# Four attention layers on one core: layer 2's transposed scores from rounded operand parts, with the maxima added in a pass of their own

## The chip, the core and the metric

The kernel runs on one core of a Trainium2 chip. The core has a matrix engine (TensorE, PE in the profile; PEld is its weight load), a vector engine (VectorE, DVE), an activation engine (ScalarE, ACT), a general engine (GpSimd, POOL) and an engine that issues DMAs (SyncE, SP). They run side by side and wait for each other through semaphores. The metric is the device time of one execution in microseconds (us); lower is better. SBUF is the on-chip memory that all engines read, PSUM the memory that TensorE writes its products to.

## The reference

Four attention layers in a row, each on x of shape (2, 128, 32, 32), that is, per image b a matrix of 128 channels by N = 1024 positions, each with a residual.

```python
# layer 0: 4 heads of 4 dims, softmax over the query positions (axis -2)
S = einsum('bhdn,bhdm->bhnm', q, k);  A = softmax(S, axis=-2)
x = gamma * (Wo @ (v A) + bo) + x
# layer 1: one head of 16 dims, v has 128 channels
x = x + gamma * (v @ softmax(q k)^T)
# layer 2: 8 heads of 16 dims; k, v from a 2x2 average pool (256 positions)
q = wq @ group_norm(x);  kvn = group_norm(avg_pool2(x));  k, v = wk @ kvn, wv @ kvn
attn = softmax(einsum('bhdq,bhdk->bhqk', q, k) * 16 ** -0.5)
x = x + wproj @ (attn v)
# layer 3: one head of 128 dims, group norm with 32 groups, biases
x = x + out_w @ softmax(q k^T * 128 ** -0.5) v + out_b
```

## The kernel before

**Steps.** The work is cut into steps that stand in one list, the plan: a string of letters, ORDER (L93 to L104), is read from left to right, and each letter takes the next step of its kind. All engines walk the same list, each doing its own part of a step, in order. So the string sets what stands behind what on every engine. The kinds:

- A: plain scores of one tile (TensorE), whose negated row maxima VectorE takes (L663 for layer 2, L666 for layer 0, L669 for layers 1 and 3).
- top: after eight A tiles the maxima are transposed (L910), copied by ScalarE (L528), and a DMA issued by SyncE puts them as rows beside or among the score operands.
- B: transposed scores of one tile with the maxima subtracted by the product itself (L918 layer 0, L923 layer 1, L929 layer 2, L933 layer 3), whose exponential ScalarE writes to one of the NP = 13 probability buffers (L539, 128x1024).
- PV4 (layers 0 and 2, four 32-column products side by side, L960, two B tiles a step) and PV1 (layers 1 and 3, L966, half a tile a step): values times probabilities, added up in one PSUM accumulator.
- N, V: q, k, v projections and the group norm steps; E, Y: sums' reciprocals (den), their broadcast (bcast), the output product (y).

**Units.** Layer 0 has four head-group units per image, layer 2 two, layers 1 and 3 one. Units of image 0 and image 1 and of neighbouring layers overlap: while image 0 changes layer, TensorE works on image 1, and the other way round.

**PSUM.** Products go to a ring of three tiles of 1024 columns (RING = 3); step n waits until the reader of step n - 3 has read. So TensorE runs at most three tiles ahead of VectorE and ScalarE.

**Number formats.** TensorE takes float32 operands (each multiply is shown as two records in the trace) or operands that were rounded on being written (fp32r; one record). A product of full accuracy can be had from rounded operands by splitting each into its rounded part and the rest. Layers 0 and 1 do so (SPLIT = (0, 1)): ScalarE writes the rounded part with a sign and mask to a staging buffer (HT, two of them, L491), VectorE adds it to the product (L630), and rows of the operand hold now the rounded part and now the rest. Layers 2 and 3 keep two copies instead: fp32r rows (RA, RB, KR2) for the A tiles, float32 rows (FA, FB, KF2) for the B tiles.

**Layer 2 in detail.** q comes in two halves of heads (g = 0, 1), each copied by ScalarE to RA or RB (L494) and by VectorE to FA or FB (L636). k is written twice per copy, once for each parity of heads, with the other parity's rows masked to zero (L472 on ScalarE to KR2, L616 on VectorE to KF2; two instructions of 512 columns each). A B tile (L929) is two float32 multiplies, one on rows 0 to 63 and one on rows 64 to 127 of the array, 512 columns each: 32 such tiles, 64 multiplies. The maxima stand in row ONE of each 32-row group of FA and FB, and masked k has a 1 there (one2k), so that the first B tile of a unit waits for their DMA (L914).

**Layers 1 and 3.** After the B tile's products a pass of its own adds the maxima: two fp32r multiplies of 64 rows and 512 columns, max_picker times max_half_rows (L941). In layer 3 the products before it are four records of 128 rows (L933).

**Vector and scalar work between layers.** From the update of x to the first A tile of layer 2 there is one chain: statistics (L755 to L762), averages over groups (L1024), the coefficients (L769 to L801), the normalized x (L580), q and k products (L845, L849, L832), the copies, the first A tile (L892).

## Time and profile before

| | |
|---|---|
| time, median of 3 runs | 370.57 us (369.66 to 370.78) |
| the profiled execution | 369.77 us, span of the core 367.6 us |
| TensorE busy | 339.6 us, 92% |
| VectorE busy | 246.5 us, 67% |
| ScalarE busy | 192.3 us, 52% |
| GpSimd busy | 52.0 us, 14% |

The span is the time from the first to the last instruction that the profile shows; the rest of the execution's time, 2.2 us, lies around it. Busy time of TensorE counts a matmul to its modelled end, so two that follow each other overlap in the trace, and the distance between the starts is what a matmul costs in a run of them.

### The profile page before, as it was taken

How to read it: one execution, taken by the hardware profiler on the slowest of the kernel's cores; microseconds unless marked ns; L12 is line 12 of the kernel's file. 1: busy time of each engine (PE TensorE's matmuls, PEld its weight loads, DVE VectorE, ACT ScalarE, POOL GpSimd, SP SyncE). 2: the span in 40 equal slices, each digit the busy share in tenths (PEclk: the TensorE clock that was granted, in tenths of full speed). 3: DMA queues.
4: the chain of work that ended last, by engine and by line, in shares of the span. 5: the costliest groups of instructions: out<-in, count | busy, mean ns of one | idle time of the engine just before them, and what ended most of it. 6: DMA issues, size and time to landing. Idle time of an engine off the chain costs nothing.

```text
span 367.6 us, 4597 instructions
## 1 busy us (share of the span) xinstructions
PE 339.6 (92%) x1766; PEld 147.7 (40%) x1766; DVE 246.5 (67%) x325; ACT 192.3 (52%) x235; POOL 52.0 (14%) x37
## 2 busy tenths in 40 slices
PE   8888989899899996899999999979999999999995
PEld 5343223333434442344343445534443343643441
DVE  2889796778889857498867437986981153890543
ACT  4454678877673477736556535237147725214310
POOL 5000000000006600000000425003210021005700
PEclk9885899999999999899999999999999999999999
DMA  7000000000000000000000000000000000000101
GB/s 295 30 0 2 0 3 1 0 2 0 2 0 2 0 0 2 2 2 2 0 4 0 2 0 0 2 0 1 3 2 4 0 0 2 0 0 2 57 0 57
DMA packets 1436, 4.43 MB, mean 12 GB/s; under 512 B 168, under 2 KB 520, under 8 KB 1288
## 3 DMA queue, kind: packets, MB, share of 16 engines
q1 hardware_dynamic: 1416, 4.15, 3.0%
q8 instruction: 14, 0.23, 0.3%
q14 instruction: 6, 0.05, 0.0%
HBM read 2.99 MB, written 1.05 MB: 11 GB/s over the span
## 4 chain that ended last, share of the span: by engine, by line
PE 74%; DVE 17%; ACT 4%; issue 4%; DVEq 0%; ACTq 0%
PE attn_acc L966 13%; PE attn_acc L960 11%; DVE neg_max L666 7%; PE products L933 7%; PE products L929 6%; PE products L918 5%; PE products L845 4%; PE products L879 4%; PE products L849 4%; PE products L857 3%; PE products L892 3%; PE products L941 2%; PE products L1015 2%; DVE neg_max L669 2%; ACT probs L539 2%
## 5 line engine op out<-in xcount | busy, mean ns | idle before, releaser
L539 ACT ACTIVATE probs<-products 128x1024 f32<-128x1024 f32 x128 | 126.9, 1025 | 86.2 <-PE products L941 50.1
L666 DVE TENSOR_REDUCE neg_max<-products 128x2 f32<-128x1024 f32 x64 | 75.9, 1219 | 14.8 <-PE products L879 14.4
L966 PE MATMUL attn_acc<-probs,v 128*128 128x512 f32 x128 | 64.0, 614 | 0.1
L960 PE MATMUL attn_acc<-probs,v 128*32 128x512 f32 x384 | 50.3, 612 | 0.1
L393 POOL TENSOR_TENSOR prob_sum<-prob_sum,probs 128x1024 f32<-128x1024 f32 x16 | 37.7, 2358 | 66.4 <-ACT probs L539 65.8
L669 DVE TENSOR_REDUCE neg_max<-products 128x1 f32<-128x1024 f32 x32 | 37.8, 1219 | 8.6 <-PE products L884 6.6
L393 POOL TENSOR_TENSOR prob_sum<-probs 128x1024 f32<-128x1024 f32 x4 | 9.4, 2360 | 229.9 <-ACT probs L539 229.9
L663 DVE TENSOR_REDUCE neg_max<-products 128x4 f32<-128x1024 f32 x32 | 37.7, 1219 | 4.1 <-PE products L892 3.6
L933 PE MATMUL products<-rows_a,rows_b 128*128 128x512 f32 x64 | 31.3, 611 | 0.5 <-ACT v L518 0.3
L966 PEld LDWEIGHTS attn_acc<-probs,v 128*128 128x128 f32 x128 | 21.8, 189 | 20.9 <-issue 17.1
L684 DVE RECIPROCAL recips<-products 128x128 f32<-128x128 f32 x10 | 9.6, 956 | 21.7 <-PE products L986 21.6
L918 PE MATMUL products<-rounded_a,q_even 64*128 64x512 f32 x64 | 16.7, 520 | 2.9 <-DVE neg_max L666 2.2
L879 PE MATMUL products<-q_even,rounded_a 64*128 64x512 f32 x64 | 16.3, 524 | 1.8 <-DVE neg_max L666 1.1
L563 ACT ACTIVATE attn_out<-attn_acc 128x512 f32<-128x512 f32 (+1 forms) x15 | 11.9, 792 | 10.8 <-PE attn_acc L960 8.2
L929 PE MATMUL products<-rows_a,k_rows 64*128 64x512 f32 x64 | 16.4, 610 | 0.4 <-DVE neg_max L663 0.4
L933 PEld LDWEIGHTS products<-rows_a,rows_b 128*128 128x128 f32 x64 | 11.2, 189 | 12.7 <-issue 11.4
L879 PE MATMUL products<-rounded_b,rounded_a 64*128 64x512 f32 x64 | 14.3, 453 | 1.0 <-ACT probs L539 0.7
L960 PEld LDWEIGHTS attn_acc<-probs,v 128*32 128x32 f32 x384 | 8.5, 109 | 16.3 <-issue 11.3
L929 PE MATMUL products<-rows_b,k_rows 64*128 64x512 f32 x64 | 14.9, 599 | 0.0
L918 PE MATMUL products<-rounded_a,rounded_b 64*128 64x512 f32 x64 | 14.2, 466 | 0.6 <-DVE neg_max L666 0.5
L941 PE MATMUL products<-max_half_rows,max_picker 64*128 64x512 f32 x64 | 14.3, 442 | 0.0
L580 ACT ACTIVATE x_norm<-x,norm_scale_shift 128x512 f32<-128x512 f32 x8 | 6.1, 806 | 13.1 <-DVE norm_scale_shift L779 13.1
(140 smaller groups left out, 388.1 us busy)
## 6 DMA issues: line engine op xcount, KB each, us to landing
w<-w_rest SPq DMA_DIRECT2D x1, 1236.5 KB, 7.6
x<-x SPq DMA_DIRECT2D x2, 512.0 KB, 4.6
tmp<-row_selector SPq DMA_DIRECT2D x1, 512.0 KB, 8.4
y<-x SPq DMA_DIRECT2D x1, 512.0 KB, 2.6
y<-x SPq DMA_DIRECT2D x2, 256.0 KB, 2.0
w<-w_first SPq DMA_DIRECT2D x1, 147.0 KB, 2.2
rounded_a<-max_rows SPq DMA_DIRECT2D x8, 4.0 KB
max_half_rows<-max_rows SPq DMA_DIRECT2D x4, 4.0 KB
```

The costliest lines, as they stand in the source:

```text
L393: engine.tensor_tensor(DS[:, :], first_in, P[:, n % NP, :], ALU.add).then_inc(den_acc, 1)
L539: nc.scalar.activation(P[:, n % NP, :], slot(s), ACT.Exp, scale=SCALE[L]).then_inc(read_act, 1)
L663: nc.vector.tensor_reduce(out=m2, in_=slot(s).rearrange("p (a i k) -> p a i k", a=2, i=2), op=ALU.max, axis=AX.X, negate=True).then_inc(re ...
L666: nc.vector.tensor_reduce(out=m[:, 2 * t:2 * t + 2], in_=slot(s).rearrange("p (a n) -> p a n", a=2), op=ALU.max, axis=AX.X, negate=True).t ...
L669: nc.vector.tensor_reduce(out=m[:, t:t + 1], in_=slot(s), op=ALU.max, axis=AX.X, negate=True).then_inc(read_dve, 1)
L879: mm = nc.tensor.matmul(slot(s)[:, halves[a]], RA[b][rows, tile], q0_parity(b, g // 2)[rows, halves[nh]], start=True, stop=True)
L918: mm = nc.tensor.matmul(slot(s)[:, halves[a]], q0_parity(b, g // 2)[rows, 128 * t:128 * (t + 1)], RA[b][rows, halves[g % 2]], start=True, ...
L929: mm = nc.tensor.matmul(slot(s)[:, halves[a]], KF2[b][rows, hp, g, 128 * kt:128 * (kt + 1)], (FA, FB)[g][b][rows, halves[half]], start=Tru ...
L933: nc.tensor.matmul(slot(s)[:, h], FB[b][:, 128 * t:128 * (t + 1)], FA[b][:, h], start=True, stop=False)
L941: mm = nc.tensor.matmul(slot(s)[:, h], pick[rows, :], MR[b][rows, :], start=False, stop=True)
L960: mm = nc.tensor.matmul(acc[32 * j:32 * j + 32, h], lhs, P[:, b_no[q] % NP, halves[a]], start=t0 == 0 if L == 0 else t0 % 2 == 0, stop=t0 ...
L966: mm = nc.tensor.matmul(acc[:, h], V13[b][:, t0, :], P[:, b_no[q] % NP, h], start=t0 == first, stop=t0 == last)
```

## The change

**Layer 2's B tiles.** SPLIT takes in layer 2. The q and k rows now hold each 16-dim head twice in its 32-row group: the rounded part and the rest. k is stored in two versions for each parity (KS[b], versions v = 0, 1), with the parts in the one and in the other order, so that the sum of both products is the whole product. A B tile is four fp32r multiplies of 64 rows and 512 columns, and then two more, max_picker times the rows of maxima (MR, MR1), which add the maxima: six instead of two, all fp32r. The wait for the maxima's DMA stands between the fourth and the fifth. The A tiles use version 0.

**Staging.** For q (each half of heads) ScalarE writes the negated rounded part to HT and VectorE adds it to the product. For k ScalarE writes four pieces of 512 columns (parity times version) instead of two, and VectorE writes four instead of two. VectorE's first waits for ScalarE's last. ScalarE waits, before it writes to one of the two HT buffers, until VectorE has read what was there two stagings before (k counts as two).

**Layer 3.** The maxima are written as one row of 1024 (row 2) instead of two half rows, and the pass that adds them is two multiplies of all 128 rows, one for each half of the columns, instead of two of 64 rows each.

**Constants.** max_picker comes by a DMA (192 KB more) and is rounded by ScalarE in the fold step, instead of being set by GpSimd.

**Buffers.** Probability buffers 12 instead of 13, output buffers 4 instead of 5.

**Order.** ORDER is a new string.

```diff
-SPLIT = (0, 1)
-NP = 13
+SPLIT = (0, 1, 2)
+PARITIES = 2
+NP = 12
-O_TILES = 5
+O_TILES = 4
...
-    "BPPBBEBPNBPBBNPPBPNNBPBABAPBAPAVAPAPAEAETNEBBABBAB"
+    "BPPBBEBBPNBBNPBPNNBBPPPPABAPBAAVAPAPAEAETNEBBBABAP"
...
-                        for p in range(2):
-                            masked = nc.scalar.activation(KR2[b][:, p, :, :].rearrange("p g n -> p (g n)"),
-                                                          slot(s)[:, 0:2 * NKV], ACT.Identity,
-                                                          scale=w("group_mask")[:, p:p + 1],
-                                                          bias=w("one2k")[:, p:p + 1])
+                        for p in range(PARITIES):
+                            at = staged.index(s) + p
+                            if at >= 2:
+                                wait_read(act, staged[at - 2])
+                            for v, h in enumerate(halves):
+                                i = PARITIES * v + p
+                                hi = nc.scalar.activation(HT[:, at % 2, h], slot(s)[:, 0:2 * NKV], ACT.Identity,
+                                                          scale=w("s2k")[:, i:i + 1])
...
-                        for p in range(2):
-                            masked = nc.vector.tensor_scalar(KF2[b][:, p, :, :].rearrange("p g n -> p (g n)"),
-                                                             slot(s)[:, 0:2 * NKV], w("group_mask")[:, p:p + 1],
-                                                             w("one2k")[:, p:p + 1], ALU.mult, ALU.add)
+                        for p in range(PARITIES):
+                            for v, h in enumerate(halves):
+                                lo = nc.vector.scalar_tensor_tensor(
+                                    out=KS[b][:, v, p, :, :].rearrange("p g n -> p (g n)"), in0=slot(s)[:, 0:2 * NKV],
+                                    scalar=w("group_mask")[:, p:p + 1] if PARITIES == 2 else 1.0,
+                                    in1=HT[:, (staged.index(s) + p) % 2, h].bitcast(F32), op0=ALU.mult, op1=ALU.add)
...
-                            mm = nc.tensor.matmul(slot(s)[:, halves[a]], KF2[b][rows, hp, g, 128 * kt:128 * (kt + 1)],
-                                                  (FA, FB)[g][b][rows, halves[half]], start=True, stop=True)
+                            for v in range(2):
+                                nc.tensor.matmul(slot(s)[:, halves[a]], KS[b][rows, v, hp, g, 128 * kt:128 * (kt + 1)],
+                                                 (RA, RB)[g][b][rows, halves[half]], start=v == 0, stop=False)
+                        if t == 0:
+                            pe.wait_ge(consts_act, 1)
+                            pe.wait_ge(maxrows_in[b], max_count(L, b, g))
+                        for a in range(2):
+                            rows = slice(WIDE * a, WIDE * a + WIDE)
+                            mm = nc.tensor.matmul(slot(s)[:, halves[a]], pick[rows, hp, :], (MR[b], MR1)[g][rows, halves[half]],
+                                                  start=False, stop=True)
...
-                            rows = slice(WIDE * i, WIDE * i + WIDE)
-                            mm = nc.tensor.matmul(slot(s)[:, h], pick[rows, :], MR[b][rows, :], start=False, stop=True)
+                            rows = slice(WIDE * i, WIDE * i + WIDE) if L == 1 else slice(0, 128)
+                            mm = nc.tensor.matmul(slot(s)[:, h], pick[rows, 0 if L == 1 else 2, :],
+                                                  MR[b][rows, 0:HALF] if L == 1 else MR[b][:, h], start=False, stop=True)
```

In the rows of order below, a name before the arrow is written and those behind it are read, sizes are partitions x columns, and x8 means eight of them in a row; v13_0 are values of image 0 in layers 1 and 3, v0_1 and v2_1 those of image 1 in layers 0 and 2.

**Place 1**, TensorE, second unit of layer 2's image 1 (its last B tiles). Before:

```order
L960 MATMUL attn_acc<-probs,v2_1 32x512 x4
L910 MATMUL products<-w2,neg_max 32x128
L929 MATMUL products<-rows_a1,k2_rows1 128x512 x6
L960 MATMUL attn_acc<-probs,v2_1 32x512 x12
L929 MATMUL products<-rows_b1,k2_rows1 128x512 x16
L986 MATMUL products<-attn_out4,w2 32x128 x8
```

After:

```order
L984 MATMUL attn_acc<-probs,v2_1 32x512 x8
L945 MATMUL products<-rounded_b1,k2_rows1 128x512 x4
L952 MATMUL products<-max_rows_odd,max_picker 128x512 x2
L945 MATMUL products<-rounded_b1,k2_rows1 128x512 x4
L952 MATMUL products<-max_rows_odd,max_picker 128x512 x2
L945 MATMUL products<-rounded_b1,k2_rows1 128x512 x4
L952 MATMUL products<-max_rows_odd,max_picker 128x512 x2
L984 MATMUL attn_acc<-probs,v2_1 32x512 x4
```

Eight B tiles in a row are now broken up by a PV4 step, and each is six instructions.

**Place 2**, TensorE, image 0's entry to layer 2, from the averages of its statistics to its first A tile (k2_rounded0 or k2_rows0); L918 and L933 are B tiles of layer 0's image 1, 128x512 x2 each. Before:

```order
L1024 MATMUL products<-mean_var,w2 128x4
L960 MATMUL attn_acc<-probs,v0_1 32x512 x8
L918 MATMUL products<-rounded_a1,rounded_b1 128x512 x2
L845 MATMUL products<-x_norm,w2 128x512
L849 MATMUL products<-x_norm,w2 128x512
L832 MATMUL products<-kv_norm,w2 128x256 x2
L918 MATMUL products<-rounded_a1,rounded_b1 128x512 x2
L960 MATMUL attn_acc<-probs,v0_1 32x512 x4
L918 MATMUL products<-rounded_a1,rounded_b1 128x512 x2
L892 MATMUL products<-k2_rounded0,rounded_a0 128x256 x4
```

After:

```order
L1048 MATMUL products<-mean_var,w2 128x4
L984 MATMUL attn_acc<-probs,v0_1 32x512 x4
L933 MATMUL products<-rounded_a1,rounded_b1 128x512 x2
L984 MATMUL attn_acc<-probs,v0_1 32x512 x4
L860 MATMUL products<-x_norm,w2 128x512
L864 MATMUL products<-x_norm,w2 128x512
L847 MATMUL products<-kv_norm,w2 128x256 x2
L933 MATMUL products<-rounded_a1,rounded_b1 128x512 x4
L984 MATMUL attn_acc<-probs,v0_1 32x512 x12
L907 MATMUL products<-k2_rows0,rounded_a0 128x256 x4
```

Three PV4 steps stand now between the k product and the first A tile, where one stood.

**Place 3**, image 1's entry to layer 2, TensorE; L933 (before) and L956 (after) are B tiles of layer 3's image 0. Before:

```order
L1024 MATMUL products<-mean_var,w2 128x4
L966 MATMUL attn_acc<-probs,v13_0 128x512
L933 MATMUL products<-rows_a0,rows_b0 128x512 x2
L941 MATMUL products<-max_half_rows0,max_picker 128x512 x2
L966 MATMUL attn_acc<-probs,v13_0 128x512
L845 MATMUL products<-x_norm,w2 128x512
L849 MATMUL products<-x_norm,w2 128x512
L832 MATMUL products<-kv_norm,w2 128x256 x2
L845 MATMUL products<-x_norm,w2 128x512
L849 MATMUL products<-x_norm,w2 128x512
L933 MATMUL products<-rows_a0,rows_b0 128x512 x2
L941 MATMUL products<-max_half_rows0,max_picker 128x512 x2
```

After:

```order
L1048 MATMUL products<-mean_var,w2 128x4
L956 MATMUL products<-rows_a0,rows_b0 128x512 x2
L964 MATMUL products<-max_rows_of0,max_picker 128x512 x2
L990 MATMUL attn_acc<-probs,v13_0 128x512
L860 MATMUL products<-x_norm,w2 128x512
L864 MATMUL products<-x_norm,w2 128x512
L847 MATMUL products<-kv_norm,w2 128x256 x2
L990 MATMUL attn_acc<-probs,v13_0 128x512 x3
L860 MATMUL products<-x_norm,w2 128x512
L864 MATMUL products<-x_norm,w2 128x512
L907 MATMUL products<-k2_rows1,rounded_a1 128x256 x4
L956 MATMUL products<-rows_a0,rows_b0 128x512 x2
```

Three PV1 steps moved in behind the k product, and the B tile of layer 3 that stood ahead of the first A tile (L892, which follows the last row of before) stands now behind it (L907). On VectorE the same place is, before:

```order
L636 COPY rows_a1<-products 128x512 x2
L616 TENSOR_SCALAR k2_rows1<-products,w1,w2 128x512 x2
L636 COPY rows_b1<-products 128x512 x2
L663 TENSOR_REDUCE neg_max<-products 128x2x2 x16
L684 RECIPROCAL recips<-products 128x128
```

and after:

```order
L642 SCALAR_TENSOR_TENSOR rounded_a1<-products,stage_hi 128x512 x2
L627 SCALAR_TENSOR_TENSOR k2_rows1<-products,w1,stage_hi 128x512 x4
L642 SCALAR_TENSOR_TENSOR rounded_b1<-products,stage_hi 128x512 x2
L678 TENSOR_REDUCE neg_max<-products 128x2x2 x16
L699 RECIPROCAL recips<-products 128x128
```

Ahead of the sixteen maxima stand eight instructions instead of six.

## Rows read from the trace of the kernel before

**Rows 1.** The page: busy time by engine; chain that ended last.

```profile
PE 339.6 (92%) x1766; PEld 147.7 (40%) x1766; DVE 246.5 (67%) x325; ACT 192.3 (52%) x235; POOL 52.0 (14%) x37
...
PE 74%; DVE 17%; ACT 4%; issue 4%; DVEq 0%; ACTq 0%
```

**Rows 2.** Windows: length; busy us (instructions) of PE, PEld, DVE, ACT, POOL; granted clock; DMA.

```profile
0.00:40.00 40.00, 34.48 (x128) 16.81 (x128) 28.56 (x36) 19.38 (x26) 4.79 (x17) 0.79 0.20 75
...
320.00:367.60 47.60, 42.86 (x149) 17.65 (x148) 21.61 (x22) 10.68 (x12) 11.76 (x5) 0.99 0.06 22
```

**Rows 3.** Timeline of PE, layer 2's last eight B tiles: start us, us, instructions.

```profile
283.21 7.14 PE L929 MATMUL products<-rows_b,k_rows 64*128 64x512 f32 x32
290.27 0.64 PE L986 MATMUL products<-attn_out,w 128*32 128x128 f32 x16
```

**Rows 4.** The same, records alive at 283.25 and at 284.0.

```profile
283.21 0.70 PE L929 MATMUL products<-rows_b,k_rows 64*128 64x512 f32 x2
...
283.74 0.59 PE L929 MATMUL products<-rows_b,k_rows 64*128 64x512 f32 x2
```

**Rows 5.** Timeline of PE, fp32r multiplies of 64 rows, a pair each row.

```profile
109.77 0.50 PE L879 MATMUL products<-rounded_b,rounded_a 64*128 64x512 f32 x2
110.11 0.39 PE L923 MATMUL products<-rounded_a,rounded_b 64*128 64x512 f32 x2
110.34 0.39 PE L941 MATMUL products<-max_half_rows,max_picker 64*128 64x512 f32 x2
110.57 0.39 PE L879 MATMUL products<-rounded_b,rounded_a 64*128 64x512 f32 x2
```

**Rows 6.** Timeline of PE, B tiles of layer 3 in the last unit.

```profile
345.39 1.98 PE L933 MATMUL products<-rows_a,rows_b 128*128 128x512 f32 x4
347.31 0.50 PE L941 MATMUL products<-max_half_rows,max_picker 64*128 64x512 f32 x2
347.74 1.99 PE L933 MATMUL products<-rows_a,rows_b 128*128 128x512 f32 x4
```

**Rows 7.** Timeline of PE, fp32r multiplies of 128 rows beside float32 ones.

```profile
224.94 1.36 PE L897 MATMUL products<-rounded_b,rounded_a 128*128 128x512 f32 x4
226.13 1.02 PE L966 MATMUL attn_acc<-probs,v 128*128 128x512 f32 x2
```

**Rows 8.** Timeline, image 0's entry to layer 2.

```profile
151.03 1.45 ACT L472 ACTIVATE k_rounded<-products,w 128x512 fp32r<-128x512 f32 x2 [1.11 <-PE products L832]
...
152.58 1.53 DVE L616 TENSOR_SCALAR k_rows<-products,w 128x512 f32<-128x512 f32 x2 [1.87 <-ACT k_rounded L472]
154.26 0.50 PE L892 MATMUL products<-k_rounded,rounded_a 64*128 64x256 f32 x4 [1.22 <-DVE k_rows L616]
```

**Rows 9.** Durations by line (ns, min/median/max): staging and copies of 512 columns.

```profile
L630 DVE SCALAR_TENSOR_TENSOR rounded_a<-products,w,stage_hi x8: 750/751/751, 7.4 to 176.8; 128x512 fp32r<-128x512 f32 x8
...
L494 ACT ACTIVATE rounded_a<-products x4: 581/593/598, 148.6 to 251.0; 128x512 fp32r<-128x512 f32 x4
...
L496 ACT ACTIVATE rounded_a<-products,w x4: 671/684/687, 220.9 to 312.1; 128x512 fp32r<-128x512 f32 x4
```

**Rows 10.** Timeline, image 1's entry to layer 2.

```profile
253.39 1.88 PE L933 MATMUL products<-rows_a,rows_b 128*128 128x512 f32 x4
253.43 1.53 DVE L616 TENSOR_SCALAR k_rows<-products,w 128x512 f32<-128x512 f32 x2 [1.03 <-ACT k_rounded L472]
...
255.54 0.40 PE L892 MATMUL products<-k_rounded,rounded_a 64*128 64x256 f32 x4
...
256.07 5.83 DVE L663 TENSOR_REDUCE neg_max<-products 128x4 f32<-128x1024 f32 x5
```

**Rows 11.** Windows with the granted clock, at both entries to layer 2.

```profile
145.00:149.00 4.00, 2.26 (x4) 1.01 (x5) 1.08 (x5) 3.22 (x5) 0.00 (x0) 0.87 0.00 0
149.00:153.00 4.00, 4.00 (x17) 1.64 (x15) 1.80 (x3) 2.75 (x5) 0.00 (x0) 0.70 0.01 2
240.00:257.00 17.00, 14.48 (x46) 6.48 (x48) 12.27 (x35) 9.05 (x14) 2.51 (x2) 1.00 0.00 1
```

More of the change, by code:

```diff
@@ L156, in build_plan, with attention_layers @@
     return [next(following[c]) for c in ORDER]
-def attention_layers(nc, x, first, rest, sel, out):
+def attention_layers(nc, x, first, rest, sel, picker, out):
     plan = build_plan()
@@ L345, in max_count @@
             order = [s for s in top_no if s[2] == b]
-            return 16 * sum(MAX_DMAS[s[1]] for s in order[:order.index(("top", L, b, g)) + 1])
+            return 16 * (order.index(("top", L, b, g)) + 1)
         def acc_free(L, b, g):
@@ L1072 @@
     group_mask = np.zeros((2, 2, GROUP, 2), np.float32)
[L1073 removed]
+    s2 = np.zeros((2, 2, 2, D2, 2, PARITIES), np.float32)
     for p in range(2):
         group_mask[:, p, :, p] = 1
[L1076 removed]
+    for v in range(2):
+        for p in range(PARITIES):
+            s2[:, slice(p, p + 1) if PARITIES == 2 else slice(0, 2), 1 - v, :, v, p] = -1
+    s2q = np.zeros((4, 2, D2, 1), np.float32)
+    s2q[:, 1] = -1
+    picker = np.zeros((2, 2, GROUP, 3, C), np.float32)
+    for p in range(2):
+        picker[:, p, 0, p] = 1
+    picker[0, 0, 2, 2] = 1
     w0o = np.zeros((4, 32, 2, 2, 32), np.float32)
```

114 lines of the change are left out of this document (60 added, 54 removed), and 1 row of the table REST.

## The prediction

> **What bounds the kernel now.** I read the page first: TensorE is busy 92% of the span and makes 74% of the chain that ended last; VectorE has 17% of that chain [rows 1]. The windows then show where TensorE is not enough of an answer: in the first 40 us it is busy 34.5 us at a granted clock of 0.79, in the last 47.6 us it is busy 42.9 us at 0.99 [rows 2]. So what TensorE is spared or given counts nearly in full from layer 2 on, except at the entries to a layer, where one chain through VectorE and ScalarE runs and TensorE lives on the other image's tiles. The change touches both: the price of B tiles, and the chain at the two entries to layer 2.
>
> **Layer 2's B tiles, removed work.** Eight B tiles (32 records, four a tile) start at 283.21 and the next step starts at 290.27 [rows 3]: 7.06 / 8 = 0.88 us a tile. In the records, two start together at 283.21 and two at 283.74 [rows 4]. The first distance, 0.53, holds a load that a wait kept back; the rest of the run is then (7.06 - 0.53) / 15 = 0.435 for a pair. So a tile is two slots of 0.43, 0.86 in a run and 0.96 after a wait.
>
> **The same, added work.** Six fp32r multiplies, three on each half of the array's rows. Pairs of that kind start at 110.11, 110.34 and 110.57, 0.23 apart, and 0.34 after the first pair, which had waited [rows 5]. If they pair up, a tile is 3 x 0.23 = 0.69 in a run and 0.34 + 2 x 0.23 = 0.80 after a wait. That is 0.16 less, times 32 tiles = **-5.1 us**. The pairing is the question, since the code gives both products of rows 0 to 63 before those of rows 64 to 127. The float32 tile answers it: there too one multiply, with both its records, stands ahead of the other half's, and yet the trace shows one record of each half starting together [rows 4]. I take three slots. Four slots, 0.92, would be +0.06 a tile; that is a rival below. The wait for the maxima moves from ahead of the tile to behind four of its multiplies; as the unit's first tile waits for a DMA, that can hide at most 0.46 in each of four units, and I count nothing.
>
> The Trainium skill ("TensorE: Matmul & The Clock Gate", Part 3, What overlaps and what doesn't) has matmuls start and end strictly in program order. By that rule a float32 tile alone would need three slots, a0, a0 with a1, a1, and the two pairs of rows 4 would not be seen; the new tile would take four slots whenever the next step is not one on half the rows (six of the 32 in the new order: 1.4 us given back). The trace speaks against the rule here, and the sum above doesn't use it.
>
> **Layer 3's maxima.** From one tile to the next it is 347.74 - 345.39 = 2.35 us [rows 6]. Four float32 records of all rows at 0.43 are 1.72, so the pass on half the rows costs 0.63, though its pair alone would be 0.23: the change between the array's two shapes costs 0.40, once in and once out. After the change both multiplies use all rows and follow each other. Four such start at 224.94 and the next step at 226.13 [rows 7]: 0.30 each with the first one's wait in it, 0.23 without. A tile is then 1.72 + 0.46 = 2.18 (2.32 by the 0.30), 0.17 less. Where the next step uses half the rows anyway (four of sixteen tiles before, two in the new order), the change of shape is only put off. I take 14 tiles x 0.17 = -2.4, plus two at +0.2: **-2.0 us**; between -2.7 and 0.
>
> **Image 0's entry to layer 2** (place 2). ScalarE writes the two k pieces from 151.03 to 152.48, VectorE from 152.58 to 154.11, and the first A tile starts at 154.26 after 1.22 us of waiting [rows 8]. Now there are four and four. For ScalarE a piece with a scale but no bias has no row: it lies between 0.593 (neither) and 0.684 (bias alone), and two such pieces overlap as those in the 1.45 do [rows 8, 9]. Four at 0.63 are 2.5, +1.05. For VectorE the same instruction as L630 is 0.751 [rows 9]; four with the overlap seen in rows 8 are 2.85, +1.3. The chain is 2.35 longer. Cover: one PV4 step, two slots of 0.43, more stands ahead of the first A tile than before (six between the update of x and that tile, for five), and is missing after it. Net **+1.5 us**. Between +0.7, if PSUM's ring lets TensorE use more of what it has, and +3, if it waits again for what it did early. One PV4 step less stands ahead of the averages (place 2), so that a gap opens there earlier; it is part of this sum.
>
> **Image 1's entry** (place 3). The k copies end at 253.43 + 1.53 = 254.96, the first A tile starts at 255.54 and the maxima at 256.07, and five of them take 5.83, some 1.13 apart [rows 10]. With the chain 2.35 longer the k rows are there at 257.3, so the A tile is 1.8 late. Ahead of it TensorE has done two PV1 steps more (1.7) and one layer 3 tile less (2.18): +0.5. Then a wait that the change adds: ScalarE stages q's second half in the HT buffer that k's first parity used, so it waits for VectorE's last k piece; VectorE's next instruction waits for that. 257.3 + 0.7 + 2 x 0.75 = 259.5 for the first of sixteen maxima instead of 256.07. Behind it wait the ring of three tiles and TensorE's A tiles; sixteen maxima at 1.13 would end at 277.6. I add 0.2 for the ring: **+2.5 us**, between +1.5 and +3.5.
>
> **Order and buffers.** Counting, in both orders, changes between steps on all rows, half the rows and 32-column groups, with layer 3's maxima taken as all rows in both: 184 and 191. Seven more at about 0.2 (half of the 0.40 above) are 1.4; half of them I take to fall where TensorE waits anyway: **+0.7**, between -1 and +2. Fewer buffers: in the new order no exponential needs a buffer whose PV step stands less than ten steps ahead of it, and no output buffer is asked for before its last reader is over 80 steps past: nothing. With one more wait of ScalarE on PV in image 0's last layer 0 tiles, 1 us at most. The larger constant DMA is issued after all that the start needs, and its rounding is one short instruction in the fold step: nothing.
>
> **The sum.** -5.1 - 2.0 + 1.5 + 2.5 + 0.7 = -2.4 us. The profiled execution would go from 369.77 to 367.4, and the median, which lay 0.8 above it, from 370.57 to **368.2 us**.
>
> **The rivals.**
> 1. *The gain is only half there.* Image 1's A tiles pace TensorE by VectorE's maxima (1.13 each), and the last B tiles by ScalarE. For it: five maxima without a gap [rows 10]. Against it: 92% busy [rows 1]. If layer 2's tiles give 2.6 instead of 5.1: 370.57 + 0.1 = 370.7 us.
> 2. *The entries cost more* (the slower side). Both are at their upper ends, 3 + 3.5 = 6.5 instead of 4.0, and the longer idleness brings the clock down. At image 0's entry TensorE was busy 2.26 of 4 us and the granted clock fell to 0.87 and then 0.70, that is, part of the time on the lower of its two levels (1.2 instead of 2.4 GHz); at image 1's entry it stayed at 1.00 [rows 11]. The price of that fall was 0.3 x 4 + 0.13 x 4 = 1.7 us. Idle a little longer at image 1's entry, and it is paid there too: -2.4 + 2.5 + 1.7 = +1.8, 372.4 us. [...] Against it: B tile and PV1 steps fill most of it.
> 3. *Four slots instead of three.* 32 x 0.23 = 7.4 more than the sum: 375.6 us. Against it speak rows 4.
> 4. *The new order hides the entries.* Places 2 and 3 show work moved to where the chain is longer; if it all counts, the +4.7 for entries and order shrink to 1: 364.5 us.
> 5. *It doesn't do what it says.* The multiplies are fp32r on rounded operands as in layers 0 and 1, whose trace rows exist; I see no way for that, and give it nothing.
>
> **How the numbers follow.** The forecast, 366.8 to 369.3, has 0.48; rival 1 has 0.23, rival 2 0.15, rival 3 0.05, rival 4 0.09. A difference under 0.3% (1.1 us) can't be told from no change. Faster by more than that are the forecast, rival 4 and a little of rival 1: 0.58. Within it is most of rival 1 and a little of rival 2: 0.23. Slower: rival 3, most of rival 2, a little of rival 1: 0.19. The range takes in half of rival 4 and rival 2: 365.0 to 372.2.
>
> **What would show it.** The B tiles of layer 2 in a run: starts of tiles 0.69 apart, records in three pairs 0.23 apart (four distances if rival 3 holds). Layer 3's tiles 2.18 apart. The four k pieces: 2.5 us on ScalarE and 2.85 on VectorE at both entries, and the first A tiles 2.35 later after the k product. On VectorE at image 1's entry a gap of about 0.7 between k's last piece and q's first. TensorE's busy time should fall by some 5 to 7 us, and its idle time rise by about 4. The prediction is wrong if the granted clock falls at a second place, if rows show four slots, or if the stretch before image 0's entry, which the change hardly touches, differs by over 1 us by the new order alone.

## The result, and the profile after

The changed kernel takes 373.3 us (median of 5 runs, 372.5 to 374.57) where before takes 369.66 (median of 5 beside them, the three runs of the first median among them): ratio 1.0092, 95% interval 1.0070 to 1.0115, some 3.4 us slower. Another six runs gave 373.84, ratio 1.0104 (1.0075 to 1.0132), which is 3.8 us. The forecast was 368.2 us and its range ended at 372.2. The profiled execution took 373.17 us with a span of 370.7, where before has 369.77 and 367.6: +3.1 in the span.

The page of the changed kernel, busy time by engine (beside rows 1):

```profile
PE 337.1 (91%) x1830; PEld 157.7 (43%) x1830; DVE 245.1 (66%) x329; ACT 194.9 (53%) x240; POOL 53.1 (14%) x35
```

TensorE is busy 2.5 us less, and idle 33.6 us (370.7 - 337.1) for 28.0 before: 5.6 more. So its work did get less, but by half or less of the 5 to 7 us that the prediction had named as a sign, and more than that turned into waiting.

**Where it went.** The table cuts the span at ends of single instructions that all these kernels have: a layer's first or last row maxima on VectorE and a layer's last exponential on ScalarE. Each column is one profiled execution. The mark (c) says that TensorE's granted clock fell once in that stage; the low clock of the first 42 us, which every trace has and which lies in stages a and b, and the fall in the last 6 us are not marked. E2's two falls straddle the ends of the stages c and e. The other columns are experiments, told below: E1 (new order, old steps), E2 (old order, new steps), E9 and E10 (new steps with k's second version copied by DMA, in the old order and in the new).

| stage, us | before | after | E1 | E2 | E9 | E10 |
|---|---|---|---|---|---|---|
| a. start to first maxima, image 0 | 12.5 | 13.5 | 13.1 | 12.5 | 13.2 | 12.6 |
| b. to the last layer 0 maxima of image 1 | 116.2 | 118.0 | 119.0 (c) | 116.6 | 117.0 | 118.7 (c) |
| c. image 0's entry, to layer 2's first maxima | 27.3 (c) | 27.1 | 26.6 (c) | 28.5 (c) | 25.8 | 26.8 (c) |
| d. to the last layer 3 maxima of image 0 | 83.2 | 82.3 | 83.2 | 83.6 | 82.3 | 82.3 |
| e. image 1's entry, to layer 2's first maxima | 18.1 | 21.3 (c) | 19.3 | 21.2 | 18.3 | 19.5 |
| f. to the last layer 2 exponential | 34.5 | 33.9 | 35.9 | 35.1 (c) | 34.0 | 34.3 |
| g. to the last layer 3 exponential | 59.4 | 59.6 | 61.7 | 58.4 | 59.4 | 59.5 |
| h. to the end | 16.4 | 15.1 | 15.3 | 16.2 | 16.2 | 15.1 |
| span | 367.6 | 370.7 | 374.0 | 372.1 | 366.2 | 368.9 |

A new order also moves work across these cuts, so single stages of kernels with different orders compare only roughly. The stages with layer 2's B tiles (d and f) gained 0.9 and 0.6 where 5.1 in all was forecast, image 1's entry lost 3.2, and stage b, before layer 2, lost 1.7 (117.96 for 116.24).

**The tiles themselves came out as forecast.** Timeline of TensorE in the changed kernel, layer 2's last unit (L945 the products, L952 the maxima):

```profile
285.52 0.63 PE L945 MATMUL products<-rounded_b,k_rows 64*128 64x512 f32 x4
285.98 0.40 PE L952 MATMUL products<-max_rows_odd,max_picker 64*128 64x512 f32 x2
286.21 0.63 PE L945 MATMUL products<-rounded_b,k_rows 64*128 64x512 f32 x4
286.67 0.41 PE L952 MATMUL products<-max_rows_odd,max_picker 64*128 64x512 f32 x2
```

286.21 - 285.52 = 0.69 a tile: three slots, for 0.88 in rows 3. Layer 3 (beside rows 6):

```profile
334.76 1.88 PE L956 MATMUL products<-rows_a,rows_b 128*128 128x512 f32 x4
336.08 1.03 PE L964 MATMUL products<-max_rows_of,max_picker 128*128 128x512 f32 x2
336.95 0.59 PE L956 MATMUL products<-rows_a,rows_b 128*128 128x512 f32 x1
```

336.95 - 334.76 = 2.19, forecast 2.18.

**Image 1's entry** (beside rows 10), VectorE and ScalarE:

```profile
256.11 2.73 DVE L627 SCALAR_TENSOR_TENSOR k_rows<-products,w,stage_hi 128x512 fp32r<-128x512 f32 x4 [1.91 <-ACT stage_hi L482]
259.71 1.29 DVE L642 SCALAR_TENSOR_TENSOR rounded_b<-products,stage_hi 128x512 fp32r<-128x512 f32 x2 [0.88 <-issue]
260.92 1.21 DVE L678 TENSOR_REDUCE neg_max<-products 128x4 f32<-128x1024 f32 x1
```

```profile
253.57 2.42 ACT L482 ACTIVATE stage_hi<-products,w 128x512 fp32r<-128x512 f32 x4 [0.17 <-PE products L847]
258.93 1.27 ACT L499 ACTIVATE stage_hi<-products,w 128x512 fp32r<-128x512 f32 x2 [2.93 <-DVE k_rows L627]
```

ScalarE's four k pieces take 2.42 (forecast 2.5), VectorE's four 2.73 (2.85). ScalarE then waits 2.93 until VectorE has read the last k piece, and VectorE stands 0.88 before q's second half (0.7). This is the wait through the staging buffer that the prediction described. At image 0's entry the same pieces and TensorE's wait, beside rows 8:

```profile
151.38 2.42 ACT L482 ACTIVATE stage_hi<-products,w 128x512 fp32r<-128x512 f32 x4 [0.18 <-PE products L847]
```

```profile
153.91 2.73 DVE L627 SCALAR_TENSOR_TENSOR k_rows<-products,w,stage_hi 128x512 fp32r<-128x512 f32 x4 [1.91 <-ACT stage_hi L482]
```

```profile
156.78 0.50 PE L907 MATMUL products<-k_rows,rounded_a 64*128 64x256 f32 x4 [1.52 <-DVE k_rows L627]
```

### The profile page after: what moved, and what is told of

The parts are those of the page before. It is cut to its first block and busy times, and to the rows that moved or that the text cites. A ratio compares the mean times of both kernels' runs of the same rounds, so it can differ in the third digit from the quotient of the medians.

```text
span 370.7 us, 4743 instructions
## 1 busy us (share of the span) xinstructions
PE 337.1 (91%) x1830; PEld 157.7 (43%) x1830; DVE 245.1 (66%) x329; ACT 194.9 (53%) x240; POOL 53.1 (14%) x35
## 5 line engine op out<-in xcount | busy, mean ns | idle before, releaser
L684 DVE TENSOR_REDUCE neg_max<-products 128x1 f32<-128x1024 f32 x32 | 37.9, 1220 | 10.2 <-PE products L899 7.0
L956 PE MATMUL products<-rows_a,rows_b 128*128 128x512 f32 x64 | 32.4, 631 | 0.8 <-DVE neg_max L678 0.6
L964 PE MATMUL products<-max_rows_of,max_picker 64*128 64x512 f32 (+1 forms) x64 | 23.0, 497 | 0.1
L699 DVE RECIPROCAL recips<-products 128x128 f32<-128x128 f32 x10 | 9.5, 954 | 19.7 <-PE products L1010 19.5
L393 DVE TENSOR_TENSOR prob_sum<-prob_sum,probs 128x1024 f32<-128x1024 f32 x8 | 9.8, 1220 | 19.1 <-POOL prob_sum L393 18.4
L933 PE MATMUL products<-rounded_a,q_even 64*128 64x512 f32 x64 | 16.0, 508 | 3.7 <-DVE neg_max L681 2.5
L933 PE MATMUL products<-rounded_a,rounded_b 64*128 64x512 f32 x64 | 14.7, 472 | 2.5 <-ACT probs L549 2.1
L956 PEld LDWEIGHTS products<-rows_a,rows_b 128*128 128x128 f32 x64 | 11.8, 194 | 12.0 <-issue 9.8
L984 PEld LDWEIGHTS attn_acc<-probs,v 128*32 128x32 f32 x384 | 8.3, 109 | 15.1 <-issue 11.8
L933 PEld LDWEIGHTS products<-rounded_a,q_even 64*128 64x128 f32 x64 | 6.5, 200 | 16.1 <-DVE neg_max L681 9.4
L964 PEld LDWEIGHTS products<-max_rows_of,max_picker 64*128 64x128 f32 (+1 forms) x64 | 9.3, 192 | 8.9 <-issue 8.7
```

Source lines behind the costliest of these rows:

```text
L393: engine.tensor_tensor(DS[:, :], first_in, P[:, n % NP, :], ALU.add).then_inc(den_acc, 1)
L684: nc.vector.tensor_reduce(out=m[:, t:t + 1], in_=slot(s), op=ALU.max, axis=AX.X, negate=True).then_inc(read_dve, 1)
L933: mm = nc.tensor.matmul(slot(s)[:, halves[a]], q0_parity(b, g // 2)[rows, 128 * t:128 * (t + 1)], RA[b][rows, halves[g % 2]], start=True, ...
L956: nc.tensor.matmul(slot(s)[:, h], FB[b][:, 128 * t:128 * (t + 1)], FA[b][:, h], start=True, stop=False)
L964: mm = nc.tensor.matmul(slot(s)[:, h], pick[rows, 0 if L == 1 else 2, :], MR[b][rows, 0:HALF] if L == 1 else MR[b][:, h], start=False, sto ...
L984: mm = nc.tensor.matmul(acc[32 * j:32 * j + 32, h], lhs, P[:, b_no[q] % NP, halves[a]], start=t0 == 0 if L == 0 else t0 % 2 == 0, stop=t0 ...
```

## The experiments

Three theories stood against each other. **A**: the longer k chains at the two entries to layer 2 cost what the tiles gain. **B**: the new order loses time by itself. **C**: layer 2's B tiles are paced by VectorE (maxima) and ScalarE (exponentials), so that a cheaper tile on TensorE gives only a part.

| | edit | median, us | ratio to before (95%) |
|---|---|---|---|
| E1 | before, new ORDER and buffers | 375.24 | 1.0139 (1.0119 to 1.0159) |
| E2 | after, old ORDER | 375.57 | 1.0165 (1.0131 to 1.0199) |
| E3 | before, layer 3's maxima by all rows | 369.26 | 0.9982 (0.9963 to 1.0000) |
| E4 | after, k's second version not made | 370.34 | 1.0001 (0.9980 to 1.0023) |
| E5 | after, one product of two left out | 370.49 | 1.0012 (0.9980 to 1.0044) |
| E6 | after, k's copies begin one parity earlier | 374.34 | 1.0096 (1.0059 to 1.0134) |
| E7 | E2 without k's second version | 368.26 | 0.9944 (0.9917 to 0.9971) |
| E8 | before, NP 12, O_TILES 4 | 370.24 | 0.9998 (0.9980 to 1.0017) |
| E9 | E2, k's second version by DMA | 368.04 | 0.9933 (0.9912 to 0.9954) |
| E10 | after, k's second version by DMA | 370.34 | 1.0007 (0.9987 to 1.0027) |
| E11 | after, layer 3's old pass | 375.95 | 1.0149 (1.0113 to 1.0184) |
| E12 | after, unedited | 373.84 | 1.0104 (1.0075 to 1.0132) |

Ratios are turned into us with 370.2 below: 0.001 is 0.37 us.

### E1 and E2: the order alone, the steps alone

E1 is the kernel before with the changed ORDER, `NP = 12` and `O_TILES = 4`; E2 is the changed kernel with the ORDER of before.

> The kernel before with the new ORDER, 12 probability and 4 output buffers, and nothing else. Theory A (the order and the buffers are nearly neutral and the entries to layer 2 cost): +0.5 to +1.5 us over the kernel before, and the first A tile of layer 2's image 1 no more than 1 us later than before. Theory B (the new order itself loses what was lost, whatever the steps are): +2.5 to +4 us, since with the dear B tiles it also has more mode changes.

> The changed steps and buffers in the old ORDER. Theory A (entries): the chains at both entries are as long as in the changed kernel (k staging 2.4 and 2.7 us, maxima of image 1 some 3.4 us later after the normalized x) and less covered, so +3 to +6 us over the kernel before. Theory B (the order loses): clearly below the changed kernel, 366 to 369 us, since the cheaper B tiles give 5 us and nothing takes them back.

E1 is 5.1 us slower than before, E2 6.1, and the two together (the changed kernel) only 3.5. So neither part is good alone: the new order costs 5.1 with the old steps, more than either theory had expected of it, and spares 2.5 with the new ones. The second number is the weaker: E2 has four runs, in two of which 3.2 and 4.0 us lie outside the span (1.9 to 2.2 in the runs of before). By the median spans, 372.8 for E2 and 371.0 and 371.95 for the two sets of the changed kernel, the order spares 0.9 to 1.8. For E1 spans and times agree (373.25 for 368.1).

The clock is not what makes the order dear. E1's run with the highest mean granted clock, 0.973, has a span of 372.4, and the runs of before at 0.970 have 367.1 to 367.6.

By the table, E1 loses in stages b, e, f and g. Stage b shows the order by itself, since none of its steps is one of the changed layers 2 and 3. Among the profiled executions that lack 8.5 us of clock in it, it takes 115.9 and 116.2 us in the old order (E7, before) and 118.0, 118.0 and 118.8 in the new (after, E12, E4). Among those that lack 9.8 to 10.2 it takes 116.6 to 117.2 in the old (E2, E3, E8, E9) and 118.3 to 119.0 in the new (E1, E5, E6, E10, E11). E2 loses 1.2 in stage c and 3.1 in e, the two entries.

### E3 and E11: layer 3's maxima

```diff
-                            rows = slice(WIDE * i, WIDE * i + WIDE)
-                            mm = nc.tensor.matmul(slot(s)[:, h], pick[rows, :], MR[b][rows, :], start=False, stop=True)
+                            rows = slice(WIDE * i, WIDE * i + WIDE) if L == 1 else slice(0, 128)
+                            mm = nc.tensor.matmul(slot(s)[:, h], (pick if L == 1 else pick3)[rows, :],
+                                                  MR[b][rows, 0:HALF] if L == 1 else MR[b][:, h], start=False, stop=True)
```

E3 makes this edit in the kernel before; E11 takes it back in the changed one.

> The kernel before with layer 3's maxima alone added by two multiplies of all rows. By the slot distances it spares 0.16 us in 12 of 16 tiles and costs 0.2 in 4: -1.2 us, of which the last unit's eight tiles (seven with -0.16) give -1.0 for certain. Theory A and B agree here: 368.2 to 369.0 us. If it is nothing or slower, TensorE's slots are not what sets the time in layer 3.

> The changed kernel with layer 3's maxima again as two half rows and the pass on half the array's rows (64 rows each), all else as changed. By the prediction's term (2.0 us for layer 3): 375.3 us, ratio 1.0146 to before. If layer 3's tiles are paced elsewhere as the single run of that part suggests (0.7): 374.0, ratio 1.011. The tiles start 2.35 apart instead of 2.19 in both cases.

In the old order the edit is worth 0.7 us, in the new one 1.7 to 2.1 (1.0149 against 1.0092 and 1.0104). E3 had been expected at 369.0 us at most and came out at 369.26. The intervals are wide, 0.7 at each end of the first and 1.3 at each end of the second. The forecast's 2.0 stands for the new order; the smaller value belongs to the old one, for which it wasn't made.

### E4 and E7: k's second version left out

```diff
-                            for v, h in enumerate(halves):
+                            for v, h in list(enumerate(halves))[:1]:
```

The edit stands in ScalarE's and in VectorE's loop, and the B product reads version 0 twice. So two k pieces of four are made on each engine, and layer 2's scores lack a part. E4 is in the changed kernel, E7 in E2.

> The changed kernel, but version 1 of k is not made and both products of a layer 2 B tile read version 0 (leaves out part of the computation): two k pieces for ScalarE and two for VectorE instead of four and four. Theory A: both entries 2.4 us shorter as chains, some -3.5 to -4.5 us in all, back to 369 to 370. Theory B: under -1.5 us, 372 or more.

> The changed steps in the old ORDER with k's version 1 not made (leaves out part of the computation), so that the entries are as short as in the kernel before and what is left of the change is its tiles. If the tiles' 5.1 + 1.2 us count in full: 364 us. Theory C: 368 to 370.5, since in the old ORDER the last eight B tiles stand in a row and ScalarE needs 0.90 for each.

E4 is 3.4 to 3.8 us under the changed kernel, E7 is 8.2 under E2 (1.0165 - 0.9944 = 0.0221). Theory A holds in both orders. The pieces left out shorten a chain by 1.2 us on ScalarE and 1.3 on VectorE (2.42 and 2.73 for four, 1.26 and 1.41 for two, as E9's rows below show for VectorE), 5.0 for both entries. In the new order, which puts more work behind them, they cost 3.4 to 3.8 of that. In the old one they cost 8.2, more than their length. By the median spans it is 6.5 (372.8 and 366.3); the rest lies outside the span, 2.4 to 4.0 us in E2's runs and 1.9 to 2.9 in E7's. The mean granted clock differs as well, 0.961 to 0.962 in E2 and 0.966 to 0.971 in E7. That is some 3 us of clock (an estimate: 0.008 x 372), more than enough for what is beyond the chains; no run separates the two.

### E5: what a cheaper B tile is worth

```diff
-                            for v in range(2):
+                            for v in range(1):
```

One of the two products of layer 2's B tiles is left out, so its scores lack a part; a tile is two slots instead of three.

> The changed kernel with one of the two products of each layer 2 B tile left out (leaves out part of the computation): two pairs instead of three, 0.23 us less in each of 32 tiles. If TensorE's slots set the time in layer 2: -7.4 us. Theory C (layer 2's tiles are paced by VectorE's maxima, 1.13 a tile, and ScalarE's exponentials, 0.90 a tile, so that a cheaper B tile gives back only part): -2 to -3.5 us, the share that the 0.16 a tile of the change itself gave.

32 tiles x 0.23 = 7.4 us of TensorE's time went, and 3.0 to 3.4 us of the kernel's (1.0012 against 1.0092 and 1.0104): 0.40 to 0.46 of it, with an interval of some 1.2 us on E5's own time. Timeline of TensorE in E5, layer 2's last unit:

```profile
288.66 0.40 PE L945 MATMUL products<-rounded_b,k_rows 64*128 64x512 f32 x2
288.89 0.40 PE L952 MATMUL products<-max_rows_odd,max_picker 64*128 64x512 f32 x2
289.47 0.50 PE L945 MATMUL products<-rounded_b,k_rows 64*128 64x512 f32 x2 [0.17 <-ACT probs L549]
289.81 0.39 PE L952 MATMUL products<-max_rows_odd,max_picker 64*128 64x512 f32 x2
290.38 0.64 PE L1010 MATMUL products<-attn_out,w 128*32 128x128 f32 x16 [0.18 <-ACT probs L549]
```

Tiles of two slots stand 0.81 and 0.91 apart here, because they wait for ScalarE to read the tile three before. The same is seen without anything left out in E9, where eight B tiles stand in a row as before (its lines are L949 and L956):

```profile
282.10 0.73 PE L949 MATMUL products<-rounded_b,k_rows 64*128 64x512 f32 x4
...
282.91 0.63 PE L949 MATMUL products<-rounded_b,k_rows 64*128 64x512 f32 x4
...
283.60 0.62 PE L949 MATMUL products<-rounded_b,k_rows 64*128 64x512 f32 x4
...
284.29 0.69 PE L949 MATMUL products<-rounded_b,k_rows 64*128 64x512 f32 x4
...
285.15 0.73 PE L949 MATMUL products<-rounded_b,k_rows 64*128 64x512 f32 x4
...
286.06 0.74 PE L949 MATMUL products<-rounded_b,k_rows 64*128 64x512 f32 x4
...
286.98 0.73 PE L949 MATMUL products<-rounded_b,k_rows 64*128 64x512 f32 x4
...
287.90 0.74 PE L949 MATMUL products<-rounded_b,k_rows 64*128 64x512 f32 x4
...
288.82 0.64 PE L1014 MATMUL products<-attn_out,w 128*32 128x128 f32 x16
```

The first tile takes 0.81 and the next two 0.69, as long as the ring of three has room; then the distance is 0.86, 0.91, 0.92, 0.92, 0.92. The run takes 6.72 us where rows 3 have 7.06, a gain of 0.34 instead of eight times 0.16. The pace of about 0.91 at its end is ScalarE's. Before the change ScalarE had that pace already, in a run of exponentials (timeline of ScalarE, before):

```profile
284.38 7.44 ACT L539 ACTIVATE probs<-products 128x1024 f32<-128x1024 f32 x8
```

Eight in 7.44 with about 1.03 of overlapping length each are (7.44 - 1.03) / 7 = 0.92 apart (an estimate), where TensorE offered one each 0.88. A row of B tiles in layer 2 was within 0.04 of ScalarE's pace. While image 1's A tiles run, the other pace holds, VectorE's: groups by line in the changed kernel, window 262.1 to 280.7, which is 18.6 us long.

```profile
L678 DVE TENSOR_REDUCE neg_max<-products 128x4 f32<-128x1024 f32 x16 | 18.6, 1217 | 1.2 <-PE products L907 1.1
```

VectorE is idle 1.2 of 18.6 us there, so the four B tiles of that stretch set no pace. Theory C holds for image 1's tiles; of image 0's sixteen the table shows only that their stage (d) gained 0.9 us, where 16 x 0.16 = 2.6 would be the full gain.

### E6: k's copies begin earlier

```diff
-                                hi = nc.scalar.activation(HT[:, at % 2, h], slot(s)[:, 0:2 * NKV], ACT.Identity,
+                                hi = nc.scalar.activation(HT[:, at % 2, h], slot(s)[:, halves[p]], ACT.Identity,
                                                           scale=w("s2k")[:, i:i + 1])
+                            if p == 0:
+                                hi.then_inc(k_first, 1)
...
```

The k product is made twice, once in each half of the tile. VectorE waits for k_first before its first parity, and q's second half waits only until that parity is read.

> The changed kernel; k's product is made twice, in both banks of its tile, so that VectorE works on the first parity while ScalarE works on the second, and q's second half waits for the first parity's piece alone. The chain is 1.2 us shorter less 0.4 for the product, and the wait ahead of the maxima at image 1's entry goes. Theory A (entries): -1.5 to -3 us. If the entries were hidden after all: within 0.5.

In its trace the chain did get shorter at image 1's entry: from ScalarE's first k piece to the end of the first maxima 263.31 - 256.40 = 6.91 us, for 262.13 - 253.57 = 8.56 in the changed kernel. VectorE then waits 0.70 for the second A tile, which stands behind a layer 3 tile on TensorE, so that 1.15 of the 1.65 are left at the second maxima. The time shows no gain where 1.5 to 3 us were expected (four runs only), and the profiled execution has three clock falls against one. Inconclusive: the gain of the chain may have gone into the falls, or into the second product of k that TensorE now makes; no run tells these apart.

### E8: the buffers

> The kernel before with 12 probability and 4 output buffers. All theories: within 0.5 us of the kernel before. If not, part of the loss is in the buffers.

Nothing, as forecast: 370.24 us beside 370.53.

### E9 and E10: k's second version by DMA

The second version is the first with the 16-row halves of each 32-row group exchanged. So it need not be staged:

```diff
...
+                if (kind, L) == ("k", 2):
+                    wait_read(sp, s)
+                    for r in range(8):
+                        to, frm = slice(D2 * r, D2 * r + D2), slice(D2 * (r ^ 1), D2 * (r ^ 1) + D2)
+                        sp.dma_start(KS[b][to, 1, :, :, :].bitcast(F32), KS[b][frm, 0, :, :, :].bitcast(F32)).then_inc(k_swapped[b], 16)
...
```

ScalarE and VectorE write the two pieces of version 0 only, k takes one staging buffer, and the first B tile of a unit waits for k_swapped.

> The changed steps in the order of before, whole computation, but k's second version is not staged: ScalarE and VectorE write two k pieces each as before the change, and SyncE issues eight DMAs (16 partitions x 4 KB each) that copy the first version with the 16-row halves of each 32-row group exchanged. k takes one staging buffer, so q's second half no longer waits for VectorE's last k piece. Theory A (the k chain at both entries is what costs; run e7 without the second version was 2.1 us under before): 2.1 under before again or up to 0.9 more by the wait of q's second half that goes, ratio 0.992 to 0.995, 367.5 to 368.5 us. Theory that e7 gained because it left work out that the DMAs now put back (TensorE waiting for them at each first B tile, or the DMAs delaying the maxima's): nearer to before, 0.998 to 1.002. The B tiles themselves in both: three pairs 0.23 apart.

> The same edit in the changed kernel with its own order. Theory A: run e4 (second version not made) was level with before, 3.0 under the changed kernel; now the same or 0.9 better: ratio 0.997 to 1.000, 369.3 to 370.5 us, and 1.5 to 2 us over the same edit in the old order, since the new order was laid out for the longer chain. Theory B (the new order costs 5 us by itself): the distance to the old order is 3 us or more.

E9 computes everything and takes 368.04 us, ratio 0.9933: 2.5 us under before and 5.9 to 6.3 under the changed kernel by the ratios (0.9933 against 1.0092 and 1.0104). E10 is level with before. Both times lie in the ranges that were expected. VectorE at image 1's entry in E9:

```profile
252.42 1.41 DVE L629 SCALAR_TENSOR_TENSOR k_rows<-products,w,stage_hi 128x512 fp32r<-128x512 f32 x2 [0.75 <-ACT stage_hi L485]
253.74 1.28 DVE L644 SCALAR_TENSOR_TENSOR rounded_b<-products,stage_hi 128x512 fp32r<-128x512 f32 x2
255.37 3.49 DVE L680 TENSOR_REDUCE neg_max<-products 128x4 f32<-128x1024 f32 x3 [0.35 <-PE products L909]
```

From the start of the k pieces to the first maxima it is 2.95 us, for 4.81 in the changed kernel (256.11 to 260.92), and q's second half follows without a gap. The eight DMAs of an image land 2.3 us after their issue in the median, the last is issued 5.6 us after the first (253.9 to 259.5), and the first B tile of the unit starts at 269.7. They hide. E10 against E9 is the new order with short chains: 1.0007 against 0.9933, 2.7 us dearer, between the 1.5 to 2 that theory A expected and the 3 of theory B. Falls of the clock don't explain it: E10's three runs at the highest mean clock, 0.974, have spans of 367.3 to 367.9, E9's eight at 0.971 to 0.972 have 363.8 to 366.2. So the new order costs time in each kernel whose entries are short. Where they are long, it earns more than it costs; by how much is less sure, as said at E2.

### E12: the changed kernel again

> The changed kernel itself, unedited, profiled and timed once more. If the falls of TensorE's granted clock belong to the program and its order (one at image 1's entry to layer 2 at 246 to 250, none at 100 to 106 and none at image 0's entry): the same places and a span within 0.5 us of 370.7. If a fall comes at one or another of three spots (100 to 106, image 0's entry near 150, image 1's entry near 248) from one execution to the next, as the runs of the new order so far differ: another set of places, and a span of 1 to 2.5 us more if there are two or three of them. Time in both: 372.5 to 374.6 us.

The profiled execution of E12 repeats the changed kernel's, span 370.7 both times and each cut of the table within 0.04 us, the clock falls included. Its other five runs have spans of 370.3 (at a mean granted clock of 0.970) and of 371.9 to 373.0 (at 0.961 to 0.963). So a program seems to have a few patterns of falls which recur (only the profiled executions show the falls themselves), and the profiled one was of the shorter kind in both cases. At the same mean clock of 0.970 the changed kernel has spans of 370.3 to 370.7 and the kernel before 367.1 to 367.6: the loss of some 3 us is there without any difference in the clock.

## Why the prediction was wrong, step by step

**Layer 2's B tiles, -5.1: mis-sized.** The slots are right (0.69 in a run, 0.80 after a wait) and rival 3 (four slots) fell. But the step "what TensorE is spared counts nearly in full from layer 2 on" fails. By E5's share of 0.40 to 0.46 it would be some 2.0 to 2.3 of 5.1, an estimate, since E5 makes the tiles cheaper still. The other way round: from E3 to E9 in the old order it is 0.9982 to 0.9933, 1.8 us, with the q staging in it. It is what rival 1 said, with its reasons (VectorE's maxima, ScalarE in the last tiles). The row which could have told it stood in the trace of before: eight exponentials in 7.44 us. 92% busy was read as 92% bound, but a busy share says nothing about the distance to the next engine's pace.

**Layer 3's maxima, -2.0.** Right in size for the new order (E11: 1.7 to 2.1), 0.7 in the old one (E3).

**The entries, +1.5 and +2.5.** The mechanism was right in each piece, with durations within 0.12 us. From ScalarE's first k piece to the first A tile of image 0 it is 156.78 - 151.38 = 5.40 us for 3.23 before (rows 8), 2.17 more where 2.35 was forecast. E10 against the changed kernel says 3.1 to 3.6 us for k's second version at both entries (1.0007 against 1.0092 and 1.0104), where 4.0 was forecast. Image 1's first maxima were forecast 3.4 after before's (259.5 for 256.07). They started at 260.92, 4.85 later, of which 1.48 was there at image 0's first layer 3 exponential already (245.58 for 244.10), so 3.4 it is. In the old order the same would have cost 8.2 (E2, E7).

**The order, +0.7: the term that failed.** It counted changes of the array's shape and nothing else. E1 measured +5.1 with the old steps, E10 against E9 +2.7 with short chains. The term was counted with layer 3's maxima taken as all rows in both orders, and E1 still has the half rows. With the edit's price in each order (1.9 in the new, 0.7 in the old) E1's number becomes 5.1 - 1.9 + 0.7 = 3.9. So the term was short by 2 to 3 us as it was defined, and by 4.4 as it enters the sum. The prediction had named what would show it: over 1 us before image 0's entry by the new order alone. Stage b is that, 1.1 us or more whichever traces with the same clock are compared, +1.7 from before to after. The new order puts work behind the chains of the new steps (places 2 and 3) and costs time elsewhere. Which exchange costs it was not settled: no run took the new order apart.

**The sum.** Against the forecast's -5.1 - 2.0 + 4.0 + 0.7 = -2.4, the runs in the new order give for the order 5.1 (E1), for layer 3 -1.9 (E11), for k's second version 3.3 (E10), and 3.5 for the whole; so -3.0 is left for layer 2's tiles and the q staging together. Each is a difference of two medians with intervals of about 1 us, so that this doesn't contradict E5's 2.0 to 2.3. Of the 5.9 us by which the forecast was wrong, 4.4 lie in the order and 2 to 3 in the tiles; the entries gave 0.7 back. This split holds for changing the order first, which fits a forecast that priced the entries with the new order's cover. Taken the other way, the new steps in the old order cost 6.1 (E2), and the order then spares 2.5.

**The rivals.** Rival 1 was true, and alone would have given 370.7. Rival 2's fall of the clock at image 1's entry came, but the one at image 0's entry went in the same execution, so that it cost nothing in sum there. In the timed runs it is in part true: seven of the changed kernel's eleven have a mean clock of 0.961 to 0.963 and spans of 371.0 to 373.0, the four at 0.970 have 370.3 to 370.7. So its median holds a further 1 us or so of low clock. Rival 4, that the new order hides the entries, has the right idea with the wrong reference: it hides them against the old order with the new steps (2.5 us by the times), not against the kernel before. **Buffers, 0:** right (E8).

The rule that was weighed (the Trainium skill, "TensorE: Matmul & The Clock Gate", Part 3, What overlaps and what doesn't: matmuls strictly in program order) is again spoken against. Within a row of tiles both readings give three distances a tile, so the last tile before a step of another shape has to tell them apart. Timeline of TensorE in the changed kernel:

```profile
293.64 0.62 PE L945 MATMUL products<-rounded_b,k_rows 64*128 64x512 f32 x4
294.11 0.40 PE L952 MATMUL products<-max_rows_odd,max_picker 64*128 64x512 f32 x2
294.43 0.65 PE L1010 MATMUL products<-attn_out,w 128*32 128x128 f32 x16
```

The next step starts 0.79 after the tile. Four distances of 0.23 would put it at 0.92 or later, and the two records of the maxima start together, as a last pair. The code gives both products of rows 0 to 63 before those of rows 64 to 127, and yet the tile takes three distances.

## What to carry to other kernels

Before a saving on the busiest engine is counted in full, compare the new pace of each run of steps with the paces of the engines that read them: here 0.69 a tile was offered to a reader that takes 0.92. A hand-made order belongs to the lengths of its chains: price it with an experiment that changes it alone, in both directions. And where a second copy of an operand is a permutation of rows of the first, a DMA between on-chip buffers takes it off both engines of the chain: that, in the order of before, made this change worth 2.5 us.

## What the runs showed of the hardware

**The clock falls once or several times within an execution, each of the same size or twice it, and small shifts move it.** The kernel before, E8 (it with fewer buffers), the changed kernel and E12, windows at the two entries, with the granted clock third from the end:

```profile
144.00:152.00 8.00, 5.93 (x21) 2.65 (x20) 3.33 (x13) 4.97 (x8) 0.00 (x0) 0.79 0.00 1
244.00:252.00 8.00, 7.50 (x21) 3.58 (x22) 4.50 (x22) 3.74 (x7) 1.44 (x1) 1.00 0.00 1
```

```profile
144.00:152.00 8.00, 5.89 (x34) 2.58 (x38) 4.10 (x21) 5.87 (x9) 0.00 (x0) 1.00 0.01 3
244.00:252.00 8.00, 7.05 (x15) 2.87 (x16) 4.14 (x22) 3.20 (x4) 0.77 (x1) 0.79 0.00 1
```

```profile
144.00:152.00 8.00, 5.81 (x30) 2.18 (x29) 4.72 (x21) 5.65 (x9) 0.00 (x0) 1.00 0.01 3
244.00:252.00 8.00, 6.48 (x15) 3.01 (x14) 4.89 (x25) 4.05 (x7) 0.00 (x0) 0.79 0.00 1
```

```profile
144.00:152.00 8.00, 5.79 (x30) 2.17 (x29) 4.71 (x21) 5.65 (x9) 0.00 (x0) 1.00 0.01 3
244.00:252.00 8.00, 6.46 (x14) 3.01 (x14) 4.87 (x25) 4.04 (x7) 0.00 (x0) 0.79 0.00 1
```

0.21 x 8 = 1.7 us of clock is missing in each fall, and so it is, once or twice over, at every such place in the fourteen traces. Between 42 and 364 us none has more than three of them; E3 and E9 have none. E8 runs before's steps in before's order and has its fall at the other entry. What a fall costs the kernel can be read from E8 against before, at the entries: 1.2 us at image 1's (stage e, 19.3 for 18.1) and 1.4 at image 0's (stage c, 27.3 for 25.9). E8's stages a and b are 1.0 us longer each; in b it lacks 1.7 us more of clock, in a the clock is the same and the cause is open. A third place is at 100 to 106, in five of eight traces of the new order and in none of six of the old. Windows of E1:

```profile
100.00:106.00 6.00, 5.59 (x30) 1.74 (x28) 4.83 (x5) 3.20 (x5) 0.00 (x0) 0.72 0.00 0
```

Ahead of such falls TensorE had been idle for part of the time (in before from 144, in the changed kernel from 244); the runs don't say how much idleness it takes.

**One kernel, several times.** E5's ten runs fall in groups by the mean granted clock: spans of 367.1 to 367.4 at 0.974 to 0.975, 368.5 to 369.1 at 0.965, 370.5 to 371.1 at 0.959 (its profiled run, 366.6 at 0.962, stands outside). The groups make up the scatter of 1% among the runs, so that a profiled execution and a median can differ by 1 us or more in what they say of an edit.
